# Graph attention logits on one Trainium2 core: the destination rows are gathered with an adding transfer onto the source rows

## The reference, cut to what matters

```python
msg_s = (s_n @ Ws_src)[src] + (s_n @ Ws_dst)[dst]
msg_v = jnp.einsum('ncx,cd->ndx', v_n, Wv_src)[src] + jnp.einsum('ncx,cd->ndx', v_n, Wv_dst)[dst]
w1 = rbf @ W_rbf
m1_s, m1_v = _cg_tp(msg_s, msg_v, y0, y1, ...)       # products with the edge's harmonics y and w1
a = (m1_s @ W_alpha)...                              # the logits
val_s = m1_s @ Ws_val                                # and the values
val_v = jnp.einsum('ecx,cd->edx', m1_v, Wv_val) * sigmoid(val_s @ Wg)
m2_s, m2_v = _cg_tp(sigmoid(val_s), val_v, y0, y1, ...)
hs, hv = m2_s @ Ws_vlin, einsum(m2_v, Wv_vlin)
```

## Time and profile before

| | |
|---|---|
| time, median of 3 runs | 6664.72 us (6659.89 to 6674.17) |
| time of the profiled execution | 6672.04 us |
| its span, first to last instruction | 6670.3 us |
| busy: PE, DVE, POOL, ACT | 4890.9, 4891.4, 4323.8, 2090.6 us |
| first and last gather of the logits | 1314.7 and 3681.8 us from the span's start |

### The profile page before, as it was taken

The page is one execution under the profiler, slowest core; times in us unless marked ns, Lnnn a source line. Parts: engine busy times, 40 slices in busy tenths (PEclk is TensorE's granted clock), DMA queues, the critical chain, the costliest instruction groups (busy, mean ns, idle before and its releaser), DMA issues. The chain is left out here.

```text
span 6670.3 us, 160444 instructions
## 1 busy us (share of the span) xinstructions
PE 4890.9 (73%) x45499; PEld 3804.3 (57%) x45500; DVE 4891.4 (73%) x10931; ACT 2090.6 (31%) x6090; POOL 4323.8 (65%) x4249
## 2 busy tenths in 40 slices
PE   5666667388888888888888577666766666687665
PEld 3444445277777777777777566544444454455444
DVE  5777775588888888888888744577777746666665
ACT  1000002166666666666666300300000011000011
POOL 5777775077767767777777155277777717777771
PEclk8888888699999999999999799888888888766787
DMA  3333332133333333333333166022222202222221
GB/s 106 88 88 89 89 89 66 40 91 94 91 91 91 90 91 91 91 90 90 93 91 91 54 184 186 27 71 70 70 70 70 72 28 68 67 67 67 67 67 34
DMA packets 401393, 545.13 MB, mean 82 GB/s; under 512 B 144934, under 2 KB 283318, under 8 KB 401180
## 3 DMA queue, kind: packets, MB, share of 16 engines
q0 software_dynamic: 193920, 331.22, 20.5%
q1 hardware_dynamic: 207388, 212.84, 11.3%
HBM read 464.79 MB, written 78.90 MB: 82 GB/s over the span
## 5 line engine op out<-in xcount | busy, mean ns | idle before, releaser
L763 POOL DMA_INDIRECT e_rows<-tab,e_idx x2424 | 2385.7, 984 | 808.8 <-issue 677.8
L1030 POOL DMA_INDIRECT acc<-tabx,a_idx x1616 | 1689.6, 1046 | 878.5 <-issue 467.0
L808 PE MATMUL e_wps<-e_w,e_hidT 64*128 64x192 f32 (+1 forms) x4848 | 803.2, 466 | 928.1 <-DVE e_hidT L877 927.2
L808 PEld LDWEIGHTS e_wps<-e_w,e_hidT 64*128 64x128 f32 x4848 | 547.1, 254 | 1137.8 <-DVE e_hidT L877 1020.7
L793 PE MATMUL e_win<-e_feat,e_ohy 128*32 128x96 f32 (+1 forms) x19392 | 1059.9, 338 | 25.1 <-DVE e_feat L871 25.0
L793 PEld LDWEIGHTS e_win<-e_feat,e_ohy 128*32 128x32 f32 x19392 | 724.7, 134 | 467.8 <-issue 322.0
L862 DVE TENSOR_TENSOR e_feat<-e_wps,e_rows 128x256 f32<-128x256 f32 x606 | 257.3, 425 | 922.5 <-DMA e_rows<-tab,e_idx 888.0
L871 DVE TENSOR_TENSOR e_feat<-e_wps,e_rows 128x384 f32<-128x384 f32 (+1 forms) x1616 | 720.0, 496 | 0.0
L1093 PE MATMUL a_c<-acc,a_buffer 128*128 128x64 f32 (+1 forms) x4848 | 624.8, 272 | 121.9 <-ACT a_buffer L1071 121.9
L1093 PEld LDWEIGHTS a_c<-acc,a_buffer 128*128 128x128 f32 (+1 forms) x4848 | 590.4, 192 | 144.0 <-issue 144.0
L782 ACT ACTIVATE e_idx<-src 128x4 int32 (+1 forms) x606 | 123.4, 205 | 1693.4 <-DMA e_rows<-tab,e_idx 1674.1
(11 more groups left out here) (245 smaller groups left out, 7839.6 us busy)
## 6 DMA issues: line engine op xcount, KB each, us to landing
h_d<-a_buffer SPq DMA_DIRECT2D x202, 322.0 KB, 2.6
s_hin<-h_d SPq DMA_DIRECT2D x202, 322.0 KB, 3.2
e_rows<-tab,e_idx POOLq DMA_INDIRECT x2424
e_ein<-in_e64T SPq DMA_DIRECT2D x202, 128.0 KB
acc<-tabx,a_idx POOLq DMA_INDIRECT x1616
a_ein<-in_e_h SPq DMA_DIRECT2D x202, 64.0 KB
e_ein<-in_e16T SPq DMA_DIRECT2D x202, 32.0 KB
tab<-p_rows SPq DMA_DIRECT2D x36, 160.0 KB
```

The source lines that it names most:

```text
L763: pool.indirect_dma_start(out=rows[:, s, t, :], out_offset=None, in_=k.tab0, in_offset=bass.IndirectOffsetOnAxis(ap=idx[:, s, t:t + 1], ax ...
L808: mm = pe.matmul(wps[:, e, 2 * u + j, 0:WC], hidT[half, edges], w2[half, :], start=True, stop=True)
L1030: pool.indirect_dma_start(out=rows[:, b, q, :], out_offset=None, in_=table, in_offset=bass.IndirectOffsetOnAxis(ap=idx[:, b, end, q:q + 1] ...
```

## The change

The four destination gathers of a group no longer fill a buffer of their own. They are issued with `compute_op=ALU.add` onto the rows of `msg` that the source gathers of the same group have filled. For that POOL waits until all four source gathers of the group have landed (`src_in`), and issues the adding gathers one step later, behind the source gathers of the next group. The buffer `far` and the DVE's sum are gone, `head` has 9 counted instructions in place of 10, and waits for `dst_in` alone. SP waits for `dst_in` alone before it loads new indices into a slot.

```diff
-    HEAD, MID, TAIL = 10, 9, 2
+    HEAD, MID, TAIL = 9, 9, 2
-        msg, far = scratch(U, TPG, XD), scratch(U, TPG, XD)
+        msg = scratch(U, TPG, XD)
@@ sync
-                            hold(sp, k, src_in[b], uses(s, i, 1) * (16 * TPG) + 16 * TPG)
                             hold(sp, k, dst_in[b], uses(s, i, 1) * (16 * TPG) + 16 * TPG)
@@ gpsimd
-                    b = s
-                    if not isinstance(g, int) or g >= U:
-                        hold(pool, k, head_ops, (g - U + 1) * HEAD)
-                    hold(pool, k, idx_in[b], i * 16 + 16)
-                    for rows, table, end, signal in ((msg, k.tabx0, 0, src_in), (far, k.tabx1, 1, dst_in)):
+                    if inside(g, n):
+                        if not isinstance(g, int) or g >= U:
+                            hold(pool, k, head_ops, (g - U + 1) * HEAD)
+                        hold(pool, k, idx_in[s], i * 16 + 16)
                         for q in range(TPG):
                             pool.indirect_dma_start(
-                                out=rows[:, b, q, :], out_offset=None, in_=table,
-                                in_offset=bass.IndirectOffsetOnAxis(ap=idx[:, b, end, q:q + 1], axis=0),
-                            ).then_inc(signal[b], 16)
-
-                rounds(pool, n, step, lo=U, U=U)
+                                out=msg[:, s, q, :], out_offset=None, in_=k.tabx0,
+                                in_offset=bass.IndirectOffsetOnAxis(ap=idx[:, s, 0, q:q + 1], axis=0),
+                            ).then_inc(src_in[s], 16)
+                    if inside(g - 1, n):
+                        b = (s - 1) % U
+                        hold(pool, k, src_in[b], uses(s, i, -1) * (16 * TPG) + 16 * TPG)
+                        for q in range(TPG):
+                            pool.indirect_dma_start(
+                                out=msg[:, b, q, :], out_offset=None, in_=k.tabx1,
+                                in_offset=bass.IndirectOffsetOnAxis(ap=idx[:, b, 1, q:q + 1], axis=0),
+                                compute_op=ALU.add,
+                            ).then_inc(dst_in[b], 16)
+
+                rounds(pool, n, step, after=1, lo=U, U=U)
@@ vector, head
-                    v.wait_ge(src_in[b], uses(s, i, 0) * (16 * TPG) + 16 * TPG)
-                    hold(v, k, dst_in[b], uses(s, i, 0) * (16 * TPG) + 16 * TPG)
-                    v.tensor_tensor(m, m, far[:, b, :, :], ALU.add).then_inc(head_ops, 1)
+                    v.wait_ge(dst_in[b], uses(s, i, 0) * (16 * TPG) + 16 * TPG)
                     hold(v, k, y_in[b], uses(s, i, 0) * 16 + 16)
                     hold(v, k, wy_ready, g + 1)
                     if not isinstance(g, int) or g >= 1:
                         hold(v, k, f_turned, g * 3)
-                    hold(v, k, head_ops, at + 1)
```

More of the change, by code:

```diff
@@ L1206, in head @@
                     v.tensor_tensor(feat[:, :, 96:160], wps[:, :, 96:160], m[:, :, 0:S], ALU.mult).then_inc(head_ops, 1)
-                    hold(v, k, head_ops, at + 3)
+                    hold(v, k, head_ops, at + 2)
                     v.tensor_reduce(red[:, :, :], vy[:, :, 0, :, :].rearrange("p t x c -> p t c x"), AX.X, ALU.add).then_inc(head_ops, 1)
@@ L1210, in head @@
                     cross(cr, vy, head_ops)
-                    hold(v, k, head_ops, at + 5)
+                    hold(v, k, head_ops, at + 4)
                     v.tensor_tensor(feat[:, :, S:96], wps[:, :, 160:192], red[:, :, :], ALU.mult).then_inc(head_ops, 1)
-                    hold(v, k, head_ops, at + 8)
+                    hold(v, k, head_ops, at + 7)
                     v.tensor_tensor(pair[:, :, :, V:2 * V], over(wps[:, :, 192:224], 2, 3), cr[:, :, :, :], ALU.mult).then_inc(head_ops, 1)
```

## The result

| | before | after |
|---|---|---|
| median | 6667.57 us (4 runs, 6659.89 to 6674.17) | 7096.81 us (4 runs, 7090.28 to 7114.85) |
| ratio | | 1.0649 [1.0631, 1.0666] |
| span of the profiled execution | 6670.3 us | 7113.0 us |

The change costs 6.5%. The forecast was 6671 and the range ended at 6920, so both were wrong. What happened is the first rival, and it cost more than the rival was priced at.

A forecast was written before the change was run, and what follows sets the result against it. The prediction took PE and ACT at their shared bank `tps` to bound the logits at 11.82 us a step. Its terms were 0 except about +6 us for the start, giving 6671 us from a median of 6664.72; range 6655 to 6920.

The forecast's parts named there:

- the first rival: Logits, POOL: adding gathers make POOL set the step; half a gather more each gives +241 us, 6906; chance 0.33.
- PE and ACT at their shared bank bound the stage; the DVE runs in its shade: Logits stage: turns and copies through `tps` set the 11.82 us step; the DVE waits for ACT once in a step.
- the ring: Logits: the cycle of PE's turns and products and ACT's copies through the one bank `tps`, 11.82 us a step.
- The DVE's sum goes: Logits, DVE: removing 202 sums of 0.818 us only lengthens the DVE's wait for ACT; term 0.
- The adding gathers come one step later: Logits, POOL: the new wait and later issue of the destination rows cost nothing in the steady state; term 0.
- The start: Group 0 of the logits: 12 gathers in place of 8, less the sum, plus landing: 5.3 - 1.0 + 2, about +6 us.
- The adding gather itself: Logits, POOL: an adding gather's extra cost lies between 0 and 1.05 us, taken below 0.23, so term 0.
- d: What one adding gather costs POOL beyond a plain one; POOL's step becomes 10.97 + 4d.
- the threshold: Logits, POOL: an extra cost of 0.23 us for each adding gather, from which POOL sets the step, at 11.88 us.
- the POOL case: Logits: POOL, with four dearer gathers a step, sets the pace; +241 us at half a gather more; chance 0.33.
- POOL becomes the bound: Logits: rival by which adding gathers stretch POOL's step to 13.05 us, 6906 in all (6809 at 0.4 each); chance 0.33.
- The rivals of the DVE and of the DMA engines: Logits: the DVE bounds after all, -179 us, 6486, chance 0.05; the DMA engines become the bound, about +910, 7580, chance 0.10.

The follow-up runs named there:

- no_sum: The kernel before without the DVE's sum, both gathers kept and the destination rows left out of the result: 6683.06 us against 6669.46, 1.0021.
- waits_first: The kernel before with PE's waits reordered at two places, the semaphore that comes last being waited for last: 6585.95 us, 0.9902.
- plain_late: The kernel after with plain gathers in place of the adding ones, overwriting the source rows; order, waits and buffers as changed: 6675.5 us, 1.0009.
- shapes: The kernel after with 128, 96, 64 and 32 rows in the four gathers of each kind, plain and adding: 6987.97 us in one run.
- two_more: The kernel before with two more plain gathers in each group, into a spare buffer that nobody reads: 7088.71 us, 1.0623.
- one_add: The kernel after with one of four destination gathers adding, the other three summed by the DVE as before: 6672.66 us against 6652.07, 1.0034.
- two_adds: The kernel after with two of four destination gathers adding, the others summed by the DVE as before: 6707.92 us, 1.0106.
- swap_third: The kernel before with PE's waits reordered and the DVE's reduction of the logits moved ahead of the gate's product, sum kept: 6573.72 us, 0.9856.

## Why the prediction was wrong, step by step

- **PE and ACT at their shared bank bound the stage; the DVE runs in its shade**: right. no_sum left the step at 11.83, and waits_first, which shortened the ring alone, moved it to 11.50. The shade was thin: there the DVE is the bound.
- **The DVE's sum goes, term 0**: right, to the last copy's start within 0.3 us (no_sum).
- **The adding gathers come one step later, term 0**: right; plain_late has it all and is at 1.0009.
- **The start, about +6 us**: right in size, by luck in one term. From the first gather to the first product it is 1336.81 - 1317.16 = 19.65 us, before 1327.70 - 1314.73 = 12.97: +6.7. Landing, for which 2 us were added, was 2.49 us against 2.17, +0.3. The adding gathers' own length, which the sum put at nothing, made 2.4 and took its place.
- **The adding gather itself, "I take d below 0.23, with little confidence"**: this is the step that failed. d is 0.73: 0.60 for an undisturbed one (shapes: mostly fixed), and 0.13 because gathers lose more to the DVE's product here. The bounds held (0 and 1.05), but for the side of the threshold no reason was given. The one row near it, the plain gather, said nothing of the add, and a threshold of 0.23 between bounds of 0 and 1.05 leaves most of the interval above it. By that interval the chance of the POOL case should have been well over a half, not 0.33.
- **The rival "POOL becomes the bound"**: right in place, sign and mechanism (two_more gives the same loss with plain gathers). Its price, 10.97 + 4 x 0.52 = 13.05, was too low twice: d was 0.73, not 0.52, which makes 13.89 and +411 us by the prediction's own formula; and the plain gathers rose from 1.046 to 1.104. The prediction's range stopped at half a gather more and so missed by 177 us. The rule that it weighed there, of "Collectives: The Full Stack" in the Trainium skill (an add needs two source reads), has the right direction for the DMA engines, as 144 packets for 48 and 2.1 times the time show. That half a gather, 0.52, came near the undisturbed 0.60 is luck: it was to come from the rows, and the rows bring 0.19 (shapes). "DMA: Bandwidth & Descriptors" in the Trainium skill, which calls the cost of more descriptors small at first, agrees with 0.8 ns a row for a plain gather and 2.2 for an adding one (shapes); that d would be near 0 does not follow from it.
- **The rivals of the DVE and of the DMA engines**: wrong, by no_sum and by 0.71 us of 2.3.
- **The lengthening by the DVE's product** had no term of its own in the sum. It was in the rows: 10.97 was more than 8 x (0.945 + 0.30) = 9.96, "and some longer ones". What made them longer was not asked, nor whether it would stay the same in another rhythm.
- The last 6 us, between the loss of the stage and of the span, lie behind the logits and were not followed up. no_sum shows that 13 us can come there without any edit to it.

The account of the step is then: 8 gathers at 0.945 with their gaps 10.0; the adding mode 4 x 0.60 = 2.4; the lengthening of all gathers 4 x 0.16 + 4 x 0.24 = 1.6, most of it by the DVE's long product; together 14.0.

## What to carry to other kernels

Before work is moved to an engine that "only issues", add up what that engine issues in a step and compare it with the bound: here POOL stood at 10.97 of 11.84 us, and an add that saved the DVE 0.8 us it did not need cost POOL 3 us it did not have. Where the price of a new operation is unknown and the threshold lies low between its bounds, forecast the far side of the threshold, or say that it is open. An engine without a pause is not by that the bound: look whether another waits for it. And at a late semaphore, wait for it last: putting the waits that are long fulfilled ahead of it was worth 1% here, more than the removed sum brought in any run on these chips.

## What the runs showed of the hardware

- An indirect gather of 128 rows of 640 bytes keeps POOL for 0.94 us, with 32 rows for 0.87, and 0.30 lie between two. With `compute_op` add it is 1.54 and 1.34.
- The adding gather makes 144 packets in place of 48 and takes 2.1 times as long on the DMA engines. The DVE starts 2.49 us after its issue has ended, against 2.34 for a plain one with the same waits (plain_late: 1335.66 to 1338.00) and 2.17 in the kernel before.
- A gather that begins in a DVE product of 1.35 us with both inputs in SBUF takes 0.36 to 0.52 us longer on average, an adding one 0.9. Cut in three, the product costs them about 0.15 and 0.20. Through this, POOL can fall into step with the DVE and keep its pace without a pause (one_add, two_adds, swap_third).
- PE starts 0.54 us after the copy's end with two fulfilled waits, each with its increment, behind the late one, and 0.14 to 0.16 us with none.
